# A two-deep instead of a three-deep ring for the attention probabilities of a Mamba, cross-attention and experts layer

## The chip, the cores and the metric

The kernel runs on one core of one Trainium2 chip. Its time is the device time of one execution in microseconds (us); lower is better. TensorE is written PE (PEld is its weight load), VectorE DVE, ScalarE ACT, GpSimd POOL and SyncE SP, as in the rows of the profile.

## What is computed

One decoder layer over x of shape 4 x 1024 x 256, all in float32, with layer norms in front of its three parts:

```python
x = x + mamba(layernorm(x))
x = x + cross_attention(layernorm(x), ctx)     # ctx: 4 x 77 x 256
x = x + experts(layernorm(x))                  # 8 experts, the top 2 of each token

# cross_attention: 16 heads of width 16, 77 keys in each batch row
q = rope(query @ Wq.T + bq)                    # 4 x 1024 x 16 x 16
k, v = ctx @ Wk.T + bk, ctx @ Wv.T + bv
attn = softmax(q @ k.T / sqrt(16), axis=-1)    # over the 77 keys
out = (attn @ v) @ Wo.T + bo
```

## The kernel before

The three parts run one after the other: `mamba_phase`, `attention_phase`, then `dispatch_phase` with `experts_phase`. Each is a block of its own with one instruction stream for each engine, and the streams meet through semaphores. Only `attention_phase` is touched.

**Units of work.** The 4096 tokens are cut into 8 chunks of 512. A chunk has two halves; a half is all 512 tokens for 8 of the 16 heads, so there are 16 halves, and a half is four tiles of 128 tokens. The scores of one tile for 8 heads are 128 x 616 numbers (8 times 77 keys). The work is written out over a slot number `g`: slot `g` belongs to tile `g`, half `g // 4`, chunk `g // 8`. Below, q is `g % 8`, so a half begins in the slots with q = 0 and q = 4.

**What each engine does in slot g, in this order.**

- PE: the scores of tile `g + 1` (L1078), the turning of one 128-row unit of an earlier half's probabilities (L1089, through `turn`), the first of the slot's jobs, the product of that unit with the values (L1101, through `times_v`), and the other jobs. In `turn` and `times_v` a half is cut into five units, each of 128 rows of (head, key) but the last, which has 104. `units(g)` says which: the first two units of half h are turned in the second slot of half h + 1, the third and fourth in the two slots after it, and **the fifth in the first slot of half h + 2**. The jobs (`jobs_at`) are the chunk's other PE work through one bank: turning the normed input (XT), the query projection (Q), turning the rotated queries (QT), the output projection (OUT), turning the second norm (NT) and the router's logits (LG, in the slots with q = 4; XT is in those with q = 0).
- ACT: `head_out` in the second slot of a half (L864), `exps` of tile `g` (8 activations of 128 x 77, L849), then `turned`, which copies the slot's turned unit from PSUM to `pT` (L858), then the copies of the jobs (L879, L884, L889) and at q = 0 and 6 two small activations for a norm.
- DVE: the sum over `exps` of tile `g - 1` and its reciprocal (`recip`, L950 and L954), the row maxima of tile `g + 1` (`maxima`, L960), then the jobs' and norms' work.
- POOL: the scaling of tile `g - 1`'s probabilities (`normalise`, L780), the rotation of the queries (L798 to L803), and the adding of the output bias.

**The ring.** `probs` holds `P_RING` halves. `exps` writes half h into place `h % P_RING`, `normalise` scales it there, and `turn` reads it. Before the first tile of half h is written, ACT waits until all five units of half `h - P_RING` have been turned:

```python
half = g // TI
if half >= P_RING and g % TI == 0:
    act.wait_ge(tr_done, UNITS * (half - P_RING) + UNITS)
```

PE waits in `scores(g)` for `exps` of tile `g - 2` (they share two pairs of PSUM banks), in `turn` for the normalised half and for the copy of the unit before the last, and in `times_v` for the copy of its own unit, made by ACT's `turned`.

Of the kernel before, what the change touches and what calls it, by code (L numbers as in the profile page):

```python
# [607 lines left out]
def attention_phase(nc, x1, ctx_t, pos, wq, wk, wv, wo, bq, bk, bv, bo, ident_c, head_mask_c, v_mask_c, inv_freq_c, gate_w,  # L608
# [25 lines left out]
    TOTAL = HT * NC  # L634
    HALVES = 2 * NC
    FIRST, LAST = -2 * HT, TOTAL + 2 * HT
    P_RING, T_RING = 3, 3

    x1c = x1.rearrange("b (c i p) d -> (b c) p i d", p=P, i=TI)
    xn2c = xn2.rearrange("(c i p) d -> c p i d", i=TI, p=P)  # L640
# [925 lines left out]
def decoder_layer(nc, a, out):  # L1566

    NB, T, DM = a["x"].shape
    N = a["a_log"].shape[1]
    NTOK = NB * T  # L1570
    E, F2 = a["gate_up_w"].shape[0], a["gate_up_w"].shape[2]
    NT = NTOK // P
    TILES = 2 * PAIRS + SINGLES
    c_rows = nc.dram_tensor("c_rows", (NB, N, T), F32).ap()
    x1 = nc.dram_tensor("x1", (NB, T, DM), F32).ap()
    xn2 = nc.dram_tensor("xn2", (NTOK + P, DM), F32).ap()
    x2 = out[0:NTOK, :].rearrange("(b t) d -> b t d", b=NB)
    mamba_phase(nc, a["x"], a["in_w"], a["conv_w"], a["xproj_w"], a["dtproj_w"], a["dtproj_b"], a["a_log"],
                a["d_vec"], a["out_w"], a["ident"], c_rows, x1)
    with nc.sbuf_tensor("logits", [P, NT, E], F32) as logits:  # L1580
        attention_phase(nc, x1, a["ctx_t"], a["pos"], a["wq"], a["wk"], a["wv"], a["wo"], a["bq"], a["bk"],
                        a["bv"], a["bo"], a["ident"], a["head_mask"], a["v_mask"], a["inv_freq"], a["gate_w"],
                        x2, xn2[0:NTOK, :], logits)
        with nc.sbuf_tensor("tables", [1, STEPS], I32) as tables, nc.sbuf_tensor("ids", [P, TILES], U32) as ids, \
             nc.sbuf_tensor("weights", [P, TILES], F32) as weights, nc.semaphore("w2_loaded") as w2_loaded, \
             nc.sbuf_tensor("w1", [P, W1_RING, DM // P, F2], F32) as w1, \
             nc.sbuf_tensor("w2", [P, E, F2 // 2 // P, DM], F32) as w2, ExitStack() as ring:
            w1_loaded = [ring.enter_context(nc.semaphore(f"w1_loaded{i}")) for i in range(W1_RING)]
            dispatch_phase(nc, logits, a["lower"], a["token"], a["expert"], a["iota"], a["gate_up_w"], a["down_w"],
                           w1, w2, w1_loaded, w2_loaded, tables, ids, weights, xn2, out)  # L1590
            experts_phase(nc, xn2, tables, ids, weights, a["gate_up_w"], w1, w2, w1_loaded, w2_loaded,
                          a["ident"], out)
# [48 lines left out]
```

## Time and profile before

| | |
|---|---|
| time, median of 3 runs | 2127.41 us (2124.16 to 2128.25) |
| the profiled execution's own time | 2127.51 us |
| its span in the profile | 2125.7 us |
| Mamba | to about 960 us |
| attention, first to last `exps` | 984 to 1258 us |
| routing and experts | from about 1280 us |
| PE busy | 1899.4 us, 89% of the span |
| DVE, ACT, POOL busy | 55%, 51%, 49% of the span |

The busy shares are averages over phases with different limits, so for a change in attention the rows between 984 and 1276 us are the ones to read. The phases don't overlap in the chain of waits: it goes back from the end through the experts' matmuls to the phase's start at 1350 us. What attention takes longer or shorter is therefore to be read as a shift of what follows it.

### The profile page before, as it was taken

The numbers are of one execution on the slowest core, as the hardware profiler recorded it, in microseconds if no ns is written. First come the engines' busy times: TensorE is split into PE (matmuls) and PEld (weight loads), VectorE is DVE, ScalarE is ACT, GpSimd is POOL, SyncE is SP. The second block draws the span as 40 slices with busy tenths as digits, with TensorE's granted clock in tenths as the row PEclk, the third lists the DMA queues.
The fourth block names the chain that finished last, engine by engine and source line by source line (L and its number), as shares of the span: only waits on it lengthen the run. The fifth ranks groups of instructions, "written<-read, shape, count | busy, mean of one in ns | idle before, by whom it ended". The sixth has DMA issues, their size and how long they took to land. (4 is left out here: it accounts for less than half of the span.)

```text
span 2125.7 us, 29061 instructions
## 1 busy us (share of the span) xinstructions
PE 1899.4 (89%) x10714; PEld 1538.6 (72%) x10714; DVE 1173.8 (55%) x1664; ACT 1086.3 (51%) x2118; POOL 1044.9 (49%) x712
## 2 busy tenths in 40 slices
PE   6889999999999998866999983799999999999998
PEld 2667777777777777654666652688888888888887
DVE  4889998999899988734656546411111111111111
ACT  3898989898989898603666650111111111111111
POOL 1687878787878787605555521322222222222121
PEclk8999999999999999978999995999999999999999
DMA  4021212121212120040000017534343434343441
GB/s 126 22 61 41 69 42 71 40 71 40 71 41 71 31 71 31 21 127 10 21 30 31 21 40 257 219 106 146 102 146 104 144 104 144 105 143 107 136 147 18
DMA packets 86637, 176.81 MB, mean 83 GB/s; under 512 B 12593, under 2 KB 57137, under 8 KB 76258
## 3 DMA queue, kind: packets, MB, share of 16 engines
q1 hardware_dynamic: 72834, 156.27, 21.5%
q0 software_dynamic: 13664, 18.69, 5.4%
q8 instruction: 87, 1.43, 0.3%
q14 instruction: 52, 0.43, 0.1%
HBM read 152.52 MB, written 22.41 MB: 82 GB/s over the span
## 5 line engine op out<-in xcount | busy, mean ns | idle before, releaser
L238 POOL TENSOR_TENSOR m_hc_ring<-m_h_ring,m_c_bc 128x1024 f32<-128x1024 f32 x256 | 606.2, 2374 | 122.6 <-DVE m_h_ring L399 104.4
L1533 PE MATMUL e_ps<-e_xT,w 128*128 128x256 f32 (+1 forms) x2560 | 502.3, 357 | 0.8 <-ACT e_xT L1460 0.8
L1533 PEld LDWEIGHTS e_ps<-e_xT,w 128*128 128x128 f32 x2560 | 441.8, 191 | 51.7 <-issue 1.1
L1444 POOL DMA_INDIRECT out<-e_y,ids x71 | 113.3, 1596 | 564.1 <-DVE e_y L1496 478.7
L490 PEld LDWEIGHTS m_ps<-m_ident,m_bxT 128*128 128x128 f32 x2048 | 234.9, 141 | 210.4 <-DVE m_h_ring L399 97.1
L283 ACT ACTIVATE m_a_ring<-m_delta,m_negA 128x512 f32<-128x512 f32 x512 | 366.1, 716 | 39.9 <-DVE m_h_ring L399 39.4
L490 PE MATMUL m_ps<-m_ident,m_bxT 128*128 128x128 f32 x2048 | 320.7, 279 | 61.9 <-DVE m_h_ring L399 56.1
L295 ACT ACTIVATE m_bxT<-m_uT,m_bT 128x512 f32<-128x512 f32 x512 | 364.4, 712 | 0.0
L1487 DVE TENSOR_TENSOR e_hT<-e_gact,e_ps 128x512 f32<-128x512 f32 x142 | 97.7, 688 | 446.4 <-ACT e_gact L1469 446.4
L399 DVE TENSOR_TENSOR_SCAN m_h_ring<-m_a_ring,m_carry,m_ps 128x512 f32<-128x512 f32 x256 | 316.5, 1267 | 27.6 <-ACT m_a_ring L283 13.1
L399 DVE TENSOR_TENSOR_SCAN m_h_ring<-m_a_ring,m_ps 128x512 f32<-128x512 f32 x256 | 303.8, 1208 | 35.5 <-ACT m_a_ring L283 12.2
L507 PE MATMUL m_ps<-m_ident,m_hc_ring 128*128 128x128 f32 x2048 | 307.6, 274 | 2.6 <-POOL m_hc_ring L238 1.7
L1469 ACT ACTIVATE e_gact<-e_ps 128x512 f32<-128x512 f32 x142 | 84.8, 597 | 415.8 <-PE e_ps L1533 415.8
L1547 PE MATMUL e_ps<-w,e_hT 128*128 x1136 | 251.8, 379 | 1.5 <-DVE e_hT L1487 1.5
L507 PEld LDWEIGHTS m_ps<-m_ident,m_hc_ring 128*128 128x128 f32 x2048 | 240.5, 141 | 4.8 <-DVE m_zT L444 2.6
L1547 PEld LDWEIGHTS e_ps<-w,e_hT 128*128 128x128 f32 x1136 | 215.1, 190 | 30.5 <-issue 1.7
L1460 ACT ACTIVATE e_xT<-e_ps 128x512 f32<-128x512 f32 (+1 forms) x40 | 22.0, 549 | 294.8 <-PE e_ps L1520 233.6
L780 POOL TENSOR_TENSOR t_probs<-t_probs,t_rtotal 128x616 f32<-128x616 f32 x64 | 77.9, 1218 | 124.8 <-DVE t_rtotal L954 124.8
L1496 DVE TENSOR_SCALAR e_y<-e_ps,weights 128x256 f32<-128x256 f32 x71 | 31.5, 480 | 194.3 <-PE e_ps L1547 194.3
L849 ACT ACTIVATE t_probs<-t_ps,t_nmax 128x77 f32<-128x77 f32 x512 | 119.2, 383 | 2.6 <-DVE t_nmax L960 2.6
L1101 PE MATMUL t_ps<-t_pT,t_v_all 128*128 128x512 f32 (+1 forms) x160 | 83.3, 618 | 14.0 <-ACT t_pT L858 13.6
L1078 PE MATMUL t_ps<-t_k_blk,t_qT 128*128 128x308 f32 x256 | 79.4, 433 | 6.9 <-ACT t_qT L884 4.9
(200 smaller groups left out, 2016.8 us busy)
## 6 DMA issues: line engine op xcount, KB each, us to landing
w<-in_gate_up_w SPq DMA_DIRECT2D x80, 1024.0 KB, 6.9
m_c_bc<-c_rows SPq DMA_DIRECT2D x32, 1024.0 KB, 6.0
w<-in_down_w SPq DMA_DIRECT2D x8, 1024.0 KB, 11.7
m_x_in<-in_x SPq DMA_DIRECT2D x8, 512.0 KB, 5.4
m_x_res<-in_x SPq DMA_DIRECT2D x8, 512.0 KB, 6.6
x<-m_x_res SPq DMA_DIRECT2D x8, 512.0 KB, 2.8
t_xa<-x SPq DMA_DIRECT2D x8, 512.0 KB, 3.9
out<-t_xa SPq DMA_DIRECT2D x8, 512.0 KB, 2.9
```

The costliest lines, as they stand in the source:

```text
L238: p.tensor_tensor(hc_ring[:, k % HC, :, :], h_ring[:, n % 2, e:e + 2, :], c_bc[:, n, :].unsqueeze(1).to_broadcast([P, 2, CT]), ALU.mult).t ...
L283: a.activation(a_ring[:, k % A_RING, :], delta[:, c % 2, e, :], ACT.Exp, scale=negA[:, e, n:n + 1]).then_inc(a_ready, 1)
L295: a.activation(bxT[:, row % BXT, i, :], uT[:, c % 2, i, :], ACT.Copy, scale=bT[:, c % 2, i, n:n + 1]).then_inc(bxT_ready, 1)
L399: v.tensor_tensor_scan(h_ring[:, n % 2, e, :], a_ring[:, k % A_RING, :], ps[:, BX + k % 2, :], initial, ALU.mult, ALU.add).then_inc(scan_d ...
L490: last = t.transpose(out[:, i * P:(i + 1) * P], src(i), ident[:])
L507: last = t.matmul(ps[:, Y + i, e * P:(e + 1) * P], hc_ring[:, k // 2 % HC, e % 2, i * P:(i + 1) * P], ident[:], is_transpose=True, start=( ...
L849: last = a.activation(dst[:, h, :], src[:, h // (HP // 2), h % (HP // 2), :], ACT.Exp, bias=nmax[:, g % 2, h:h + 1])
L1444: nc.gpsimd.indirect_dma_start(out=out, out_offset=bass.IndirectOffsetOnAxis(ap=ids[:, tile:tile + 1], axis=0), in_=y[:, s % 2, i, :], in_ ...
L1469: nc.scalar.activation(gact[:, k % 2, :], gu_bank(s, g, 0), ACT.Gelu).then_inc(g_ready, 1)
L1487: nc.vector.tensor_tensor(h_out(s, g), gact[:, k % 2, :].rearrange("p (f t) -> p f t", f=n), gu_bank(s, g, 1).rearrange("p (f t) -> p f t" ...
L1533: last = t.matmul(gu_bank(s, g, which)[:, f * wide:(f + 1) * wide], w1[:, s % W1_RING, c, lo:lo + P], xT[:, s % 2, c, 0:wide], start=(c == ...
L1547: last = t.matmul(ps[:, Y_BANK + s % 2, i * D:(i + 1) * D], hT[:, s % 2, f, i * P:(i + 1) * P], w2[:, bass.ds(e, 1), f, :].rearrange("p a ...
```

## The change

The ring of half-chunk probabilities has two places instead of three. The buffer `probs`, the place that `exps`, `normalise` and `turn` use for a half, and the count on which ACT waits in `exps` all follow from this number; nothing else in the program changes. The buffer is smaller by 4 x 616 x 4 = 9856 bytes in each partition.

```diff
-    P_RING, T_RING = 3, 3
+    P_RING, T_RING = 2, 3
```

The functions that read it are these:

```python
def probs_of(g):
    return probs[:, g // TI % P_RING, g % TI, :].rearrange("p (h m) -> p h m", m=M)
...
            def exps(g):
                act.wait_ge(max_done, g + 1)
                half = g // TI
                if half >= P_RING and g % TI == 0:
                    act.wait_ge(tr_done, UNITS * (half - P_RING) + UNITS)
...
                    last = t.transpose(ps[0:n, T_BANK + k % 2, i * P:(i + 1) * P],
                                       probs[:, h % P_RING, i, u * P:u * P + n], ident[:])
```

## Rows read from the trace of the kernel before

**Rows 1.** The page: its span, and two of the rows over 40 slices.

```profile
span 2125.7 us, 29061 instructions
...
PE   6889999999999998866999983799999999999998
...
PEclk8999999999999999978999995999999999999999
```

**Rows 2.** Busy time by stretch; the last columns are the granted clock and DMA.

```profile
984.00:1020.00 36.00, 29.50 (x130) 19.54 (x129) 23.09 (x49) 27.16 (x105) 22.89 (x17) 0.99 0.00 1
...
1054.00:1089.00 35.00, 32.46 (x161) 23.23 (x160) 23.03 (x54) 22.28 (x81) 19.94 (x16) 1.00 0.09 31
```

**Rows 3.** Waits of PE from 984 to 1260: total us, times, longest.

```profile
PE t_ps L1101 <- ACT t_pT L858: 12.1, 21, 1.0
...
PE t_ps L1034 <- POOL t_q_rot L803: 1.6, 1, 1.6
PE t_ps L1034 <- DVE t_xn L945: 1.2, 5, 0.2
```

**Rows 4.** Timeline of ACT, around a slot with q = 4 and one with q = 0.

```profile
1096.73 1.83 ACT L849 ACTIVATE t_probs<-t_ps,t_nmax 128x77 f32<-128x77 f32 x8
1098.39 0.66 ACT L858 ACTIVATE t_pT<-t_ps 128x512 f32<-128x512 f32 x1
...
1099.35 1.92 ACT L849 ACTIVATE t_probs<-t_ps,t_nmax 128x77 f32<-128x77 f32 x8
1101.74 0.60 ACT L858 ACTIVATE t_pT<-t_ps 104x512 f32<-104x512 f32 x1 [0.47 <-PE t_ps L1089]
1104.38 0.60 ACT L864 ACTIVATE t_oT<-t_ps 128x512 f32<-128x512 f32 x1 [2.05 <-PE t_ps L1101]
...
1117.84 1.91 ACT L849 ACTIVATE t_probs<-t_ps,t_nmax 128x77 f32<-128x77 f32 x8
1120.21 0.60 ACT L858 ACTIVATE t_pT<-t_ps 104x512 f32<-104x512 f32 x1 [0.47 <-PE t_ps L1089]
```

**Rows 5.** Timeline of PE, around the same two slots.

```profile
1099.10 1.12 PE L1101 MATMUL t_ps<-t_pT,t_v_all 128*128 128x512 f32 x2 [0.99 <-ACT t_pT L858]
1100.07 1.20 PE L1078 MATMUL t_ps<-t_k_blk,t_qT 128*128 128x308 f32 x4
1101.10 0.60 PE L1089 MATMUL t_ps<-t_ident,t_probs 128*104 128x128 f32 x4
1101.54 1.85 PE L1067 MATMUL t_ps<-t_gw,t_xn2T 128*128 128x8 f32 x16
1103.24 1.10 PE L1101 MATMUL t_ps<-t_pT,t_v_all 104*128 104x512 f32 x2
1104.18 1.20 PE L1078 MATMUL t_ps<-t_k_blk,t_qT 128*128 128x308 f32 x4
...
1119.58 0.60 PE L1089 MATMUL t_ps<-t_ident,t_probs 128*104 128x128 f32 x4
...
1120.88 1.11 PE L1101 MATMUL t_ps<-t_pT,t_v_all 104*128 104x512 f32 x2
```

**Rows 6.** Timeline of ACT: the 104-row copy in halves 2 and 15.

```profile
1012.65 0.60 ACT L858 ACTIVATE t_pT<-t_ps 104x512 f32<-104x512 f32 x1 [0.47 <-PE t_ps L1089]
...
1244.90 0.60 ACT L858 ACTIVATE t_pT<-t_ps 104x512 f32<-104x512 f32 x1 [0.47 <-PE t_ps L1089]
```

**Rows 7.** Timeline of PE: the 104-row product in halves 2 and 15.

```profile
1013.30 1.13 PE L1101 MATMUL t_ps<-t_pT,t_v_all 104*128 104x512 f32 x2 [0.25 <-ACT t_pT L858]
...
1246.40 1.10 PE L1101 MATMUL t_ps<-t_pT,t_v_all 104*128 104x512 f32 x2
```

**Rows 8.** Timeline of DVE: the sum that follows the exps of 1099.35.

```profile
1104.19 0.78 DVE L950 TENSOR_REDUCE t_total<-t_probs 128x8 f32<-128x616 f32 x1
```

**Rows 9.** The chain of waits, at the experts' start and just after.

```profile
1357.43 6.62 PE e_ps L1533 x16
...
1364.49 13.81 PE e_ps L1533 x64
```

## The prediction

> **What bounds the kernel now.** I read the page first, for its slices. PE is near full in Mamba and in the experts, and attention, which is slices 19 to 24 or so, is full as well, at a granted clock of full speed [rows 1]. Then I split attention by stretches. In its steady part PE is busy 32.46 of 35 us while ACT has 22.28, DVE 23.03 and POOL 19.94 [rows 2]: PE sets the pace, its order is fixed, and what ACT loses costs only where PE then stands still. So the third view is what PE waits for. It is little: 12.1 us on ACT's copies of turned units in the whole of attention, 1.6 us once on POOL, 1.2 us in five times on DVE [rows 3]. Last I read the timelines of ACT and PE side by side around the two slots in which a half begins [rows 4, 5], since the changed wait stands there and nowhere else. They are the argument.
>
> **What the change does.** No instruction is added or removed. `exps` for the first tile of half h now waits until the fifth unit of half h - 2 has been turned, instead of the fifth of half h - 3. The fifth unit of half h - 2 is turned in this very slot, the first of half h: PE does it behind the scores of tile g + 1. The wait of before was met four slots earlier. Three facts of the code decide what it costs. ACT issues in order, and behind the waiting `exps` stands `turned`, the copy of that same fifth unit. PE issues in order too, and its `times_v` for the fifth unit waits for this copy, with the next scores behind it. And PE's turning of the unit doesn't depend on the waiting `exps` (the scores of tile g + 1 need only those of tile g - 1), so there is no deadlock, and it happens as early as before.
>
> **Step 1, when the exps can start.** In the q = 4 slot PE turns the fifth unit at 1101.10 for 0.60 us [rows 5], and ACT, which waits for it today with the copy, starts at 1101.74 [rows 4]. The exps of this slot start at 1099.35 today. With the change it is they that wait for the same event, so they start at 1101.74, 2.39 us later; in the q = 0 slot at 1120.21 instead of 1117.84, 2.37 us later.
>
> **Step 2, when the copy is done.** Eight exps take 1.66 us to the start of what follows them (1096.73 to 1098.39), and from the start of a copy behind exps to PE's product are 0.71 us (1098.39 to 1099.10) [rows 4, 5]. Call X the time at which the 104-row copy starts today. The product can then start at X + 1.66 + 0.71 = X + 2.37.
>
> **Step 3, how late PE is.** With q = 0 the product starts today at 1120.88, which is X + 0.67: PE loses 1.70 us. With q = 4 it starts at 1103.24, X + 1.50, because the logits job L1067 stands between and takes PE 1.7 us [rows 4, 5]: it covers 0.83 us of the wait, and PE loses 0.87. If that cover were gone it would be 1.7 as well. Chunk 1 shows that: it has no logits job in its q = 4 slot, since LG belongs to the chunk two before.
>
> **Step 4, what is behind it.** Behind the late product PE has the next scores, today 0.94 us after the product's start (1103.24 to 1104.18) [rows 5]. They need the slot's exps, which end at 1101.74 + 1.83 = 1103.57, well before 1105.05: no second wait. ACT's next work is `head_out`, which waits for the product's end today with 2.05 us of idle time [rows 4]; it is late by PE's loss and by no more. In the q = 0 slot the second XT turn stands behind the product, and it needs the first XT copy; that follows the unit's copy on ACT by some 0.5 us, so it ends before PE has finished the product. DVE's sum over these exps stands at 1104.19 today behind other work [rows 8], later than 1103.57, so in the q = 4 slot it doesn't move; in the q = 0 slot it moves a little and the next maxima wait for the later scores anyway. POOL scales behind DVE and has no one waiting within a slot. So every engine moves by PE's loss, and the next half meets the same picture, as it has before: today's pattern repeats from chunk to chunk within 0.4 us.
>
> **Step 5, how often.** The wait exists for halves 2 to 15, 14 times. I took X and the product's start for all 14; the first is 1012.65 and 1013.30, the last 1244.90 and 1246.40 [rows 6, 7]. In eight of them the difference is 0.65 to 0.67 us (all seven with q = 0, and the q = 4 slot of chunk 1), in six it is 1.50 (the q = 4 slots of chunks 2 to 7). The sum is 8 x 1.70 + 6 x 0.87 = 13.6 + 5.2 = 18.8 us.
>
> **What could be given back, what added.** PE's waits on DVE and POOL shrink where those engines gain a lead from PE's delay: at most 1.2 + 1.6 = 2.8 us in all [rows 3], but the one POOL wait stands in the last slot of chunk 0, ahead of the first affected slot, and the DVE waits of 0.24 us stand ahead of the late product in the same slot, where the wait is covered already. I take nothing off. A group of exps is 1.92 us long where it overlaps a copy before it and 1.83 otherwise [rows 4]; if the longer one held, 14 x 0.09 = 1.3 us are to be added. That bounds the sum by 16.0 and 20.1. The shorter buffer moves the addresses behind it, and no row shows a cost for an address: nothing. Mamba and the experts don't change, and each phase starts when the one before has ended, so attention's loss is the kernel's.
>
> **Against the profiled execution** (2127.51 us: the span of 2125.7 [rows 1] and 1.8 around it; the median of the runs is 0.1 lower) this gives 2127.5 + 18.8 = 2146.3 us, 0.9% slower. What a measurement of this kernel can tell from no change is about 0.2%, 4.3 us.
>
> **The rivals.**
>
> *Absorbed, so not slower.* ACT has 12 us of idle time in 35, and its 0.47 + 2.05 us of waiting in the q = 4 slot are more than the 2.39 by which the exps are late [rows 2, 4]. If the copy were made in time for PE all the same, the time would stay 2127. It decides if the copy is ahead of the exps, or ACT's copy has slack of over 2.4 us against PE. Against it: the program has the copy behind the exps, and PE starts the product 0.67 us after the copy's start in the q = 0 slot, no slack at all. Only the six covered slots could go this way: 2127.5 + 13.6 = 2141. A rule speaks for this rival: the Trainium skill, "Trainium Kernel Development and Optimization", section Best Practices, tells one to double-buffer. It says so of DMA over compute, and two places would be enough by it, with a time of 2127; no row of before shows two places at work, and the reader of this ring needs a half for more than one half's time.
>
> *The whole stall on PE.* If PE had to wait for the late exps and not only for the copy, each place would cost about the 2.4 us by which the exps start late: 14 x 2.4 = 33.6, 2161 us. Step 4 speaks against it, with 1.5 us to spare (1103.57 against 1105.05).
>
> *The clock.* PE's new idle times, about 1.7 us each beside what is there, could bring its granted clock down from 2.4 to 1.2 GHz. 16 matmuls of the experts took 6.62 us at their start, 0.41 each, and 64 took 13.81 later, 0.22 each [rows 9]; matmul time run at the lower level so costs about 0.9 of itself more. If a tenth of attention's matmul time fell there (0.93 of the 240 us or so of its steady part [rows 2], so 22 us), 20 us come on top: 2166. Against it: the first stretch of attention has PE busy for 29.50 of 36 us and a clock of 0.99 [rows 2]. The changed chunk would have 32.5 of about 39, the same share. The Trainium skill, "TensorE: Matmul & The Clock Gate", section on the second HAM failure mode, warns of just such frequent short idle times between groups of matmuls; by it the time would be this rival's, and by the rows of the first stretch it is not.
>
> *The edit does nothing* (the wait is met already) would again be 2127. It can't be: the event it names is the one ACT waits for today with the copy, 0.47 us long [rows 4], behind 1.9 us of exps.
>
> **How the numbers follow.** The forecast, a loss of 16 to 20 us by the late copy: 0.85. Absorbed, wholly or in the covered places: 0.05, of which 0.02 near 2127 and 0.03 near 2141. The whole stall: 0.05. The clock: 0.05. The time is the likeliest case's, 2146. Its terms reach from 2143.5 to 2147.6, the runs of before spread by 4 us, and the covered places may go either way by 5; 2140 to 2152 takes these in and leaves the whole stall and the clock out. Of no change within 0.2% there is the 0.02 of full absorption and a little more; of faster, only what I may have overlooked. Faster 0.01, same 0.03, slower 0.96.
>
> **What the profile after would show.** Step 1: waits of ACT's exps (L849) on PE L1089, 14 in number and 2.3 to 2.8 us long (less 0 where ACT was waiting before), about 33 us in all, where today there are none on it. Step 2: the 104-row copy right behind the exps with no wait of its own. Step 3: PE L1101's wait on ACT's copy up from 12.1 to about 12 + 19 = 31 us, with eight waits of some 1.7 to 2.4 us and six of about 0.7 to 0.9. Step 4: L1078 doesn't wait for the exps, and the period of a chunk goes from 36.6 or 36.9 to about 39.3. Clock 1.00 throughout. The prediction is wrong if PE waits for L849, if the clock falls, or if other waits of PE shrink by several microseconds.

## The result, and the profile after

The changed kernel takes 2163.23 us (median of 4 runs, 2161.17 to 2164.59) against 2126.62 us (4 runs): 1.0172 times the time before, 95% interval 1.016 to 1.0184, 36.6 us slower. The forecast was 2146.3 us with a range of 2140 to 2152. The direction was right, and the forecast loss of 18.8 us was half of the one that came.

The page of the changed kernel, against [rows 1]:

```profile
span 2160.1 us, 29062 instructions
...
PE   5889999999999988767888884699999999999998
...
PEclk8999999999999999878999996899999999999999
```

The span is 34.4 us longer. One number shows where: the exps of attention (L849), from first to last start.

```profile
L849 ACT ACTIVATE t_probs<-t_ps,t_nmax x512: 307/352/472, 981.7 to 1290.5; 128x77 f32<-128x77 f32 x171
```

That is 308.8 us, and it was 984.3 to 1256.3, 272.0 us, before: 36.8 us more, the whole loss. Mamba ended 2.6 us earlier in this execution. From here on I call this length the **exps' span**; it leaves out what varies in the other phases.

What ACT waited for, then PE, from 984 to 1290 us of the changed kernel (total us, times, longest):

```profile
ACT t_pT L858 <- PE t_ps L1089: 34.6, 23, 3.0
ACT t_probs L849 <- PE t_ps L1089: 32.2, 14, 2.8
...
ACT t_probs L849 <- DVE t_nmax L960: 2.6, 3, 1.1
```

```profile
PE t_ps L1101 <- ACT t_pT L858: 28.4, 30, 2.5
PE t_ps L1078 <- ACT t_qT L884: 4.1, 6, 0.7
PE t_ps L1078 <- ACT t_probs L849: 2.0, 2, 1.6
```

The second row is new: 14 waits of the exps on the turning of the fifth unit. PE's wait on the copies has gone from 12.1 us [rows 3] to 28.4, and nothing else in PE's list grew. That makes 16.3 us, not 36.8. (The waits ahead of the fourteen 104-row products add up to 19.6 us where they were 1.6; PE's other waits on copies grew shorter.) The other half is in no wait. It is in the last columns of the busy time by stretch (against [rows 2]):

```profile
984.00:1020.00 36.00, 28.56 (x121) 19.25 (x122) 20.12 (x44) 24.07 (x93) 22.85 (x17) 0.95 0.00 1
1020.00:1054.00 34.00, 27.96 (x114) 18.61 (x113) 19.77 (x48) 18.09 (x66) 16.59 (x15) 0.94 0.05 16
...
1089.00:1123.00 34.00, 30.40 (x127) 21.42 (x128) 16.86 (x41) 20.01 (x72) 17.00 (x13) 0.85 0.05 16
1123.00:1158.00 35.00, 31.14 (x143) 21.66 (x141) 20.02 (x49) 18.42 (x67) 17.68 (x17) 0.95 0.09 31
```

The granted clock, 0.99 and 1.00 in the stretches of [rows 2], is 0.85 to 0.95 here. The timelines of ACT and of PE in the q = 4 slot that answers to the one of [rows 4, 5] show both halves of the loss:

```profile
1107.76 1.82 ACT L849 ACTIVATE t_probs<-t_ps,t_nmax 128x77 f32<-128x77 f32 x8
1109.41 0.66 ACT L858 ACTIVATE t_pT<-t_ps 128x512 f32<-128x512 f32 x1
1109.89 0.67 ACT L889 ACTIVATE t_xn2T<-t_ps 128x512 f32<-128x512 f32 x1
1112.82 1.83 ACT L849 ACTIVATE t_probs<-t_ps,t_nmax 128x77 f32<-128x77 f32 x8 [2.26 <-PE t_ps L1089]
1114.49 0.65 ACT L858 ACTIVATE t_pT<-t_ps 104x512 f32<-104x512 f32 x1
```

```profile
1112.56 1.85 PE L1067 MATMUL t_ps<-t_gw,t_xn2T 128*128 128x8 f32 x16
1115.19 2.08 PE L1101 MATMUL t_ps<-t_pT,t_v_all 104*128 104x512 f32 x2 [0.78 <-ACT t_pT L858]
1117.06 2.26 PE L1078 MATMUL t_ps<-t_k_blk,t_qT 128*128 128x308 f32 x4
1119.11 1.92 PE L1089 MATMUL t_ps<-t_ident,t_probs 128*128 128x128 f32 x8
1120.82 2.33 PE L1041 MATMUL t_ps<-t_wo,t_oT 128*128 128x256 f32 x8
1122.99 1.88 PE L1101 MATMUL t_ps<-t_pT,t_v_all 128*128 128x512 f32 x4
```

The exps wait 2.26 us, the copy of the 104-row unit comes behind them, and PE's product waits 0.78 us behind the logits job, as forecast. Then the product takes 2.08 us where it took 1.10, the scores 2.26 where they took 1.20 [rows 5], and from this product to the next are 7.80 us (1115.19 to 1122.99). The same kernel has the same work with no slower matmul 165 us later: 4.61 us (1280.52 to 1285.13), behind the same 0.78 us of waiting:

```profile
1280.52 1.12 PE L1101 MATMUL t_ps<-t_pT,t_v_all 104*128 104x512 f32 x2 [0.78 <-ACT t_pT L858]
1281.48 1.20 PE L1078 MATMUL t_ps<-t_k_blk,t_qT 128*128 128x308 f32 x4
...
1285.13 1.88 PE L1101 MATMUL t_ps<-t_pT,t_v_all 128*128 128x512 f32 x4
```

Cut at the wait, the stretches of the first of these slots read:

```profile
1105.00:1112.00 7.00, 6.02 (x28) 3.94 (x27) 3.95 (x8) 3.29 (x11) 4.51 (x5) 1.00 0.05 18
1112.00:1114.40 2.40, 2.40 (x22) 2.19 (x19) 0.80 (x1) 1.58 (x8) 2.32 (x3) 1.00 0.00 0
1114.40:1115.20 0.80, 0.02 (x2) 0.01 (x1) 0.75 (x3) 0.74 (x3) 0.69 (x1) 0.80 0.00 0
1115.20:1118.60 3.40, 3.40 (x6) 1.84 (x6) 0.99 (x3) 1.30 (x5) 2.22 (x2) 0.50 0.00 0
```

PE ran at 2.4 GHz up to the wait, stood idle for 0.78 us, and ran at 1.2 GHz (0.50) when its work came. This is the rival that I had given 0.05.

### The profile page after: what moved, and what is told of

It reads as the page before. It is cut to its first block and busy times, and to the rows that moved or that the text cites. A ratio compares the mean times of both kernels' runs of the same rounds, so it can differ in the third digit from the quotient of the medians.

```text
span 2160.1 us, 29062 instructions
## 1 busy us (share of the span) xinstructions
PE 1917.7 (89%) x10714; PEld 1550.0 (72%) x10714; DVE 1168.1 (54%) x1664; ACT 1085.7 (50%) x2118; POOL 1043.9 (48%) x712
## 5 line engine op out<-in xcount | busy, mean ns | idle before, releaser
L849 ACT ACTIVATE t_probs<-t_ps,t_nmax 128x77 f32<-128x77 f32 x512 | 117.5, 358 | 34.8 <-PE t_ps L1089 32.2
L1101 PE MATMUL t_ps<-t_pT,t_v_all 128*128 128x512 f32 (+1 forms) x160 | 90.4, 665 | 30.6 <-ACT t_pT L858 30.5
L960 DVE TENSOR_REDUCE t_nmax<-t_ps 128x8 f32<-128x616 f32 x64 | 50.9, 795 | 90.0 <-PE t_ps L1078 89.8
## 6 DMA issues: line engine op xcount, KB each, us to landing
w<-in_down_w SPq DMA_DIRECT2D x8, 1024.0 KB, 11.9
```

The source lines that it names most:

```text
L849: last = a.activation(dst[:, h, :], src[:, h // (HP // 2), h % (HP // 2), :], ACT.Exp, bias=nmax[:, g % 2, h:h + 1])
L1101: t.matmul(ps[:, O_BANK, :], v_all[0:n, b, u, h % 2 * P:(h % 2 + 1) * P], pT[0:n, k % T_RING, :], start=(u == 0), stop=(u == UNITS - 1)).t ...
```

## The experiments

Two theories. **The clock**: of the 36.8 us, some 19 are PE's idle time behind the late copy, and the rest is matmul work that takes longer at the lower clock because of that idle time. **Waiting alone**: the slow matmuls are a symptom that costs nothing, or something else in the change (the smaller buffer, the moved addresses, a wait in a place that I had not priced) makes the other half. All ratios are to runs of the kernel before on the same chip (its medians there: 2126.47, 2126.90 and 2127.58 us). The median is over all executions of a run, the exps' span is that of the one execution that was profiled.

| run | median us | ratio (95% interval) | exps' span us |
|---|---|---|---|
| before | 2126.62 | | 272.0 |
| the change | 2163.23 | 1.0172 (1.016 to 1.0184) | 308.8 |
| wait only, three places | 2161.55 | 1.0161 (1.0144 to 1.0178) | 305.2 |
| wait in even halves | 2146.29 | 1.0087 (1.007 to 1.0105) | 289.3 |
| wait in odd halves | 2136.33 | 1.0047 (1.003 to 1.0063) | 281.1 |
| spare transposes, 5 behind logits | 2154.06 | 1.0124 (1.0107 to 1.014) | 301.2 |
| spare transposes, 12 behind logits | 2145.3 | 1.0089 (1.0072 to 1.0105) | 293.0 |
| copy first, two places | 2138.43 | 1.0051 (1.0034 to 1.0068) | 281.6 |
| copy first, three places | 2135.66 | 1.0036 (1.002 to 1.0051) | 280.9 |
| units earlier, two places | 2131.52 | 1.0022 (1.0013 to 1.0032) | 274.4 |
| units earlier, three places | 2129.9 | 1.0014 (1.0005 to 1.0024) | 274.3 |
| units earlier and late, two places | 2122.07 | 0.9978 (0.9969 to 0.9988) | 266.6 |

**Is it the wait or the buffer?** Three places, and the wait of two:

```diff
-                if half >= P_RING and g % TI == 0:
-                    act.wait_ge(tr_done, UNITS * (half - P_RING) + UNITS)
+                if half >= 2 and g % TI == 0:
+                    act.wait_ge(tr_done, UNITS * (half - 2) + UNITS)
```

> Three places in the ring as before, but exps waits for the fifth unit of half h - 2 as with two. If the loss comes from the wait (its own 18.8 us and a lower clock behind it), 2163 us, as with the change, granted clock about 0.95 in attention. If the smaller buffer or the moved addresses have a part in it, less: between 2127 and 2150 us.

2161.55 us, and ACT's waits are the same 14 and 32.2 us:

```profile
ACT t_probs L849 <- PE t_ps L1089: 32.2, 14, 2.8
```

The interval overlaps that of the change. The buffer's size and the addresses behind it have no part that shows. The exps' span is 3.6 us shorter than with the change though the exps' waits are the same, and the clock accounts for that: here it fell behind nine of the 14 waits, at 1.3 to 1.7 us each, in the changed kernel behind ten, one of them at 3.2 us.

**One place at a time.** The same edit for even halves alone, then for odd ones (with `half % 2 == 1`); the other halves keep the wait of three places.

```diff
-                if half >= P_RING and g % TI == 0:
-                    act.wait_ge(tr_done, UNITS * (half - P_RING) + UNITS)
+                if half >= (2 if half % 2 == 0 else 3) and g % TI == 0:
+                    act.wait_ge(tr_done, UNITS * (half - (2 if half % 2 == 0 else 3)) + UNITS)
```

> The early wait for even halves alone (7 waits, the q = 0 slots), three places. If each wait costs PE its idle time and, by itself, a stretch at the lower clock: 7 x (1.70 + 1.3) = 21 us, 2148 us, and this loss and that of the odd halves add up to the 36.6 us of both. If the clock falls only where several waits come close together, the idle time alone: 11.9 us, 2139 us, clock 1.00.

> The early wait for odd halves alone (7 waits, the q = 4 slots), three places. If each wait brings its own stretch at the lower clock: 1.7 + 6 x 0.87 + 7 x 1.3 = 16 us, 2143 us. If the clock falls only where several waits come close together: 6.9 us, 2134 us, clock 1.00.

The even halves cost 17.3 us of the exps' span, the odd ones 9.1, together 26.4 against 33.2 of both in the wait-only run. Neither expectation fits, since each took the clock to fall behind all waits or behind none. Idle time alone would be 11.9 and 6.9 us. In the run with the even waits the clock fell behind four of the seven, in the one with the odd waits behind a single one, the 2.48 us of half 3. Four falls at 1.3 to 1.7 us and one at 1.7 bring the two sums to 17.6 and 8.6 us, near the 17.3 and 9.1 measured. The six waits of 0.79 us behind a logits job (waits of the odd halves) brought no fall when they stood alone. With both kinds in the kernel most of them did. So a fall isn't the price of one wait; it depends on what else stands around it. The kernel before says the same: PE waited 0.99 us in it ahead of the product of 1099.10 [rows 5], and its clock was 1.00 from 1089 to 1123.

**Is the lower clock a cause?** The decisive test gives PE more to do. The change is kept, and in each of the 14 waits PE turns the identity into the empty bank for turned units, which nothing reads:

```diff
                 for kind, c, i in todo[:1]:
                     job(kind, c, i)
+                if g % TI == 0 and 2 <= g // TI < HALVES:
+                    spare = (UNITS * (g // TI - 2) + 5) % 2
+                    for _ in range({2: 17, 3: 20, 14: 20}.get(g // TI, 12 if g % HT == 0 else 5)):
+                        t.transpose(ps[:, T_BANK + spare, 0:P], ident[:], ident[:])
                 for h, u in units(g):
                     times_v(h, u)
```

> The changed kernel with 5 to 20 spare 128-column transposes on PE in each of the 14 waits, into an empty PSUM bank, which nothing reads. They fill most of the new idle time. If half of the loss is the clock, it stays at 1.00 in attention and the time is 2127 + 19 = 2146 us. If the whole loss is waiting and the lower clock costs nothing, the time stays at 2163 us or rises by what the transposes overrun.

2154.06 us: 7.6 of the 36.8 us of exps' span are back (9.2 us by the medians; the profiled execution was the slowest of the four), not the 18 that the clock theory wants. The timeline says why. The clock fell no more behind the even halves' waits nor behind that of half 3, and behind all six waits that follow a logits job it still did:

```profile
1110.65 1.85 PE L1067 MATMUL t_ps<-t_gw,t_xn2T 128*128 128x8 f32 x16
1112.36 0.74 PE L1118 MATMUL t_ps<-t_ident 128*128 128x128 f32 x5
1113.28 1.44 PE L1101 MATMUL t_ps<-t_pT,t_v_all 104*128 104x512 f32 x2 [0.18 <-ACT t_pT L858]
1114.51 2.26 PE L1078 MATMUL t_ps<-t_k_blk,t_qT 128*128 128x308 f32 x4
```

PE stands idle for only 0.18 us here, and the clock falls all the same: the length of the last gap doesn't decide it. Each of the six costs 1.7 us: from the 104-row product with q = 4 to the next with q = 0 are 21.10 us where the clock falls, and 19.4 in the runs or halves where it doesn't. Six times 1.7 is 10.2, and with PE's own 19 us this is the loss of 29.2. So I let 12 stand in place of 5 in these slots (and 14 to 22 in the others), more than the wait holds:

> As the run with spare transposes, but 12 instead of 5 in the six waits behind the logits job, behind which alone the clock still fell there, and 14 to 22 in the others. 12 take about 1.3 us and overrun these waits by some 0.5 us: 6 x 0.5 = 3 us, and 1 to 2 us in the others. If the rest above the idle time is the clock, it holds at 1.00 and the time is 2127 + 19.5 + 4.5 = 2151 us at most, less than with 5 transposes (2154) though PE has more to do. If spare work only costs, it is 2154 + 5 = 2159 us.

2145.3 us. Seven transposes more in each of six slots and one or two more in the others, and by the medians the kernel is 8.8 us faster than with 5 (all executions of 2144.57 to 2145.6 against 2150.86 to 2158.44) and 17.9 us faster than with none. ACT's waits are unchanged, and the clock holds (waits of ACT, then PE's timeline, then stretches):

```profile
ACT t_probs L849 <- PE t_ps L1089: 32.2, 14, 2.8
```

```profile
1106.89 1.85 PE L1067 MATMUL t_ps<-t_gw,t_xn2T 128*128 128x8 f32 x16
1108.60 1.51 PE L1118 MATMUL t_ps<-t_ident 128*128 128x128 f32 x12
1109.94 1.02 PE L1101 MATMUL t_ps<-t_pT,t_v_all 104*128 104x512 f32 x2
1110.80 1.20 PE L1078 MATMUL t_ps<-t_k_blk,t_qT 128*128 128x308 f32 x4
```

```profile
1020.00:1054.00 34.00, 31.89 (x165) 23.23 (x164) 19.70 (x47) 19.54 (x71) 19.37 (x19) 1.00 0.05 16
1089.00:1123.00 34.00, 32.20 (x162) 23.11 (x161) 17.23 (x39) 20.68 (x75) 18.86 (x15) 1.00 0.09 31
```

This settles the split. With the clock held, the exps' span is 293.0 us, 21.0 over the kernel before. The 12 transposes overrun the wait by 0.42 us in each of six slots (from the product with q = 0 to this one are 20.28 us against 19.86 with 5), and 0.1 of it comes back in the interval behind (19.32 us against 19.41 in the changed kernel behind 1074.57, where its clock held): 2 us in all. That leaves 19.0 us for the waits; the forecast's sum for them was 18.8. The other 18 us of the change are the clock, and the changed kernel's own timeline agrees: against the same intervals where the clock held, its ten falls cost 1.3 to 2.1 us each in nine cases and 3.2 in one (22.61 against 19.41), 17.7 us together.

**Is the order on ACT the cause of the 18.8?** Two places, but the copy of the fifth unit stands before the exps:

```diff
+                if g % TI == 0:
+                    for h, u in units(g):
+                        turned(h, u)
                 if 0 <= g < TOTAL:
                     exps(g)
-                for h, u in units(g):
-                    turned(h, u)
+                if g % TI:
+                    for h, u in units(g):
+                        turned(h, u)
```

> Two places, but in the first slot of a half ACT copies the turned fifth unit before it runs the exps instead of after. If the loss is that the copy stands behind the waiting exps, the q = 4 slots lose nothing. In the q = 0 slots the XT copy still stands behind the exps: 6 x 1.2 us, and 0.7 us in halves 3 and 14, 8.6 us in all, 2135 us, up to 2141 us with some lower clock. If instead PE or DVE has to wait for the late exps themselves, it stays near 2160 us.

> The copy of the fifth unit before the exps, with three places. ACT works in order, so the exps behind the copy start after the fifth unit is turned with three places as with two: the time is that of the same order with two places, 2138 us within 4. If the third place were worth something of its own, it would be nearer to 2127 us.

The exps' span is 281.6 us with two places and 280.9 with three, 9.6 and 8.9 over the kernel before, where 8.6 was worked out. The exps start even later in this order, behind the copy, and PE no longer waits 0.8 us behind the logits job. What is left of the loss stands mainly where it was expected. Six of the seven waits of this row, of 1.09 us each, are PE's on the XT copy behind the exps in q = 0 slots, where the kernel before has none on it (the edit moves the later lines of the kernel by 4):

```profile
PE t_ps L1038 <- ACT t_xnT L883: 7.2, 7, 1.1
```

The two whole-kernel medians, of two chips, are 2.8 us apart with intervals that overlap; beside 0.7 us between the exps' spans I take the rest to be variation of runs. In this order the third place buys nothing in attention, since the copy makes the exps wait in any case.

**Two places without the wait.** Last I moved the event itself: the fifth unit is turned a slot earlier, in half h + 1, and a half's place is free before the next but one begins.

```diff
-            found = [(half - 2, 4)] if at == 0 else [(half - 1, 0), (half - 1, 1)] if at == 1 else [(half - 1, at)]
+            found = [[], [(half - 1, 0), (half - 1, 1)], [(half - 1, 2), (half - 1, 3)], [(half - 1, 4)]][at]
```

> Two places, and PE's units are spread differently: units 0 and 1 in a half's second slot, 2 and 3 in the third, 4 in the fourth, none in the first slot of the half after. The exps then wait for something that was done a slot before. If the wait in that slot is the whole cause, the exps' waits on L1089 vanish and the time is that of the same order with three places, about 2127 us give or take 10 for the new order. If two places cost anything else, it is slower than with three places.

> The same spreading of the units with three places, for comparison: within 0.2% of the run with two places if the wait was the whole cause of the change's loss; 2117 to 2137 us, since the new order itself may move PE's waits.

The exps' spans are 274.4 and 274.3 us, the medians 0.08% apart, and no wait of the exps on L1089 is left in either. Two places cost nothing that shows where the unit is turned in time. A third spreading puts units 3 and 4 together in the last slot (`[(half - 1, 2)], [(half - 1, 3), (half - 1, 4)]` for the last two entries):

> Two places, units 0 and 1 in a half's second slot, 2 in the third, 3 and 4 in the fourth. As with the other spreading the exps of a new half find their place free: no wait of exps on L1089, clock 1.00, and 2120 to 2137 us. If it is below 2127 us, it beats the kernel before with a smaller buffer.

2122.07 us, 0.9978 (0.9969 to 0.9988), faster, with the smaller buffer, than the kernel before and than the changed one. With three places this spreading was not run. PE's wait on the copies is less than half of the 12.1 us of [rows 3]:

```profile
PE t_ps L1101 <- ACT t_pT L858: 5.3, 11, 1.3
```

## Why the prediction was wrong

**Steps 1 and 2 held.** 14 waits of the exps, 32.2 us in all against about 33 forecast. In the slot shown, the copy starts 1.67 us after the exps and PE's product 0.70 us after that; the forecast had 1.66 and 0.71.

**Step 3 and step 5 held as far as they went.** PE waits 1.59 us with q = 0 and 0.78 us behind the logits job, and 2.03 to 2.47 us in the three slots in which it had waited 0.25 to 0.69 us for this copy before; what the waits cost with the clock held is 19.0 us against 18.8. The logits job is the cover that step 3 names.

**Step 4 held for the waits.** L1078 waits for the exps 2.0 us in two times, as before, so the whole stall didn't come. Its 2161 us lies nearer to the measured 2163 than the clock's 2166 does; only the waits and the granted clock tell the two apart. Nothing was given back either: the 1.6 and 1.2 us on POOL and DVE are still there. But its last sentence, that every engine moves by PE's loss, leaves out what PE's matmuls themselves cost behind the idle time.

**The step that failed is the one on the clock**: "The changed chunk would have 32.5 of about 39, the same share." I took the 0.99 granted in a stretch with PE busy for 29.50 of 36 us [rows 2] as evidence that a chunk with the same share keeps its clock. It is an average over 36 us, and it says nothing on where in it the idle time lies. At 30.40 busy of 34, a larger share though swollen by the slow matmuls, the changed kernel was granted 0.85. So the sum got no term for the clock, and the runs show one of about 18 us, half of the 36.6. The chunk's length shows it too: the intervals in which the clock held add up to 39.3 us (19.86 and 19.41), as forecast, and those with falls to 42.3 (21.21 and 21.11). The rival had a price of 20 us near the measured 18, but its tenth of the matmul time was assumed and came from no row, so that this was near is luck; what the text had was the mechanism, and a wrong comparison gave it a chance of 0.05. The page that I weighed there ("TensorE: Matmul & The Clock Gate" of the Trainium skill, the section "A second HAM failure mode: psum-queue depth-cycling") warned of frequent short idle times between groups of matmuls. The runs agree with its direction: with 14 waits of 0.8 to 2.5 us unfilled the clock fell behind ten of them, and with the waits filled it fell behind none.

**Open.** Why the clock falls behind one wait and not behind another of the same length isn't settled. In the changed kernel itself it fell behind four of the six waits of 0.78 us but not behind those of 1074.57 and 1280.52. In the run with 5 spare transposes it fell behind the six waits after a logits job, in the one with 12 behind none, and with the odd waits alone behind none of the six. That the logits job ahead of the wait has a part in it is suggested by the place of those six in the run with 5; the run with the odd waits alone speaks against its being enough, and no run took the job away.

## What to carry to other kernels

A ring's depth is worth what its first blocked instruction holds up: find the event that frees the place, the slot it falls in, and who stands behind the waiting instruction in order. Here it was a copy that another engine needed, and moving the freeing event by one slot made the smaller ring free, and with a better spreading faster than the larger one. Where the engine that sets the pace is PE, price its new idle time twice, as time lost and as matmuls behind it at the lower clock, and don't let a mean clock or a mean busy share over many microseconds argue the second price away. A few spare matmuls in the gap are a quick test of it: if more work makes the kernel faster and the granted clock is back at 1.00, it was the clock. Too few can fail to show it, as the run with 5 did.

## What the runs showed of the hardware

An idle time of PE of only 0.78 us, in work that was granted 1.00 up to it, was followed by a stretch at 0.50 that made 4.61 us of work take 7.80; a typical fall cost 1.3 to 1.7 us. With 5 spare transposes in the gap an idle time of 0.18 us was followed by a fall, and with the odd waits alone six of 0.79 us were not. 12 spare transposes of 128 columns in place of 5 in six such gaps, with one or two more in the other eight, made the kernel 8.8 us faster.
